# A layered transformer in one launch: expert row sends each followed by a copy, feed-forward weights quantised inside the expert stage, causal masks written by ScalarE

## What is computed

```
x = x + 0.5 * experts(ln(x))        # 8 routed experts, top 2 of them, and 2 shared; silu(x w1) * (x w3), then w2; hidden 256
x = x + attention0(ln(x))           # 16 heads of 8, 4 sequences of 1024, causal mask
x = x + 0.5 * experts(ln(x))        # the same weights
x = x + 0.5 * fp4_ffn(ln(x))        # gate, up, down with inner 352
x = x + attention1(ln(x))           # 16 heads of 64
x = x + 0.5 * fp4_ffn(ln(x))

def fp4_quant_dequant(x):           # blocks of 16 along the last dim; used on activations and on weights
    scale = max(max(|block|) / 6, 1e-12)
    return nearest_grid(|block| / scale) * sign(block) * scale   # grid 0 0.5 1 1.5 2 3 4 6
```

## Time and profile before

| what | us |
|---|---|
| median of three runs | 2107.71 |
| the profiled execution's own time | 2103.85 |
| its span in the profile | 2102.1 |
| of it: experts m1 (11.4 to 340) | 328.6 |
| attention0 (340 to 1016) | 676.0 |
| experts m2 (1016 to 1354.6) | 338.6 |
| feed-forward weights (1354.6 to 1373.5) | 18.9 |
| feed-forward f1 and the next norm (1373.5 to 1630) | 256.5 |
| attention1 (1630 to 1948) | 318.0 |
| feed-forward f2 and the end | 154 |

### The profile page before, as it was taken

How to read it: one execution, slowest core, us unless ns; L and a number is a source line. 1 busy time by engine, 2 the same in 40 slices (tenths; PEclk the granted TensorE clock), 3 DMA queues, 4 the chain that set the end, 5 groups by cost and what they waited for, 6 DMA issues and landing times. The chain is left out here.

```text
span 2102.1 us, 31391 instructions
## 1 busy us (share of the span) xinstructions
PE 1707.6 (81%) x10505; PEld 1173.3 (56%) x10505; DVE 1345.0 (64%) x2565; ACT 876.7 (42%) x1530; POOL 620.4 (30%) x669
## 2 busy tenths in 40 slices
PE   3987783999999999999399788257579999999475
PEld 2656661544544444443276676135347888888254
DVE  5534356877777777774463344579887666663796
ACT  2323331466666666667132333123224444444232
POOL 2355453211111011111226654213213333334132
PEclk9989996999999999999679898679879999999798
DMA  6022321111011111110402132100100000000000
GB/s 221 26 61 62 107 61 59 28 35 27 21 36 26 31 26 26 33 29 12 179 13 65 58 88 82 66 0 0 42 1 1 1 0 0 0 0 1 0 0 41
DMA packets 47705, 82.35 MB, mean 39 GB/s; under 512 B 10948, under 2 KB 32900, under 8 KB 46532
## 3 DMA queue, kind: packets, MB, share of 16 engines
q1 hardware_dynamic: 38500, 62.09, 10.3%
q0 software_dynamic: 9088, 18.76, 2.7%
HBM read 43.19 MB, written 31.22 MB: 35 GB/s over the span
## 5 line engine op out<-in xcount | busy, mean ns | idle before, releaser
L1824 DVE TENSOR_REDUCE z_parts<-z_pM 128x4 f32<-128x512 f32 x576 | 380.3, 687 | 144.6 <-PE z_pM L1576 78.3
L1745 ACT ACTIVATE z_Pr<-z_pE 128x512 f32<-128x512 f32 x576 | 326.4, 599 | 198.6 <-PE z_pE L1600 190.1
L1600 PE MATMUL z_pE<-z_QM,z_QK 128*128 128x512 f32 x576 | 265.1, 465 | 0.9 <-ACT z_Pr L1745 0.9
L1576 PE MATMUL z_pM<-z_KM,z_Q 128*128 128x512 f32 x576 | 247.7, 432 | 14.1 <-DVE z_parts L1824 7.6
L1928 POOL TENSOR_SCALAR_AFFINE_SELECT z_Pr<-z_Pr 128x512 f32<-128x512 f32 x128 | 81.5, 637 | 541.2 <-ACT z_Pr L1745 540.3
L1389 POOL TENSOR_TENSOR a_pm<-a_Pn,k_mask 128x512 f32<-128x512 f32 x128 | 132.4, 1059 | 271.4 <-PE a_pT L1227 153.4
L456 POOL DMA_INDIRECT slot_results<-m_yq,m_xq x156 | 150.8, 967 | 129.1 <-ACT m_yq L639 97.8
L1600 PEld LDWEIGHTS z_pE<-z_QM,z_QK 128*128 128x128 f32 x576 | 108.8, 190 | 134.3 <-ACT z_Pr L1745 103.0
L421 POOL DMA_INDIRECT slot_rows<-m_XN,m_dest x128 | 124.2, 970 | 162.7 <-issue 64.7
L1613 PE MATMUL z_pO<-z_Pr,z_V 128*9 128x512 f32 (+3 forms) x1536 | 159.7, 488 | 0.4 <-POOL z_Pr L1928 0.3
L1576 PEld LDWEIGHTS z_pM<-z_KM,z_Q 128*128 128x128 f32 x576 | 108.3, 188 | 80.5 <-DVE z_parts L1824 71.6
(11 more groups left out here) (286 smaller groups left out, 3769.5 us busy)
## 6 DMA issues: line engine op xcount, KB each, us to landing
slot_rows<-in_c_pad SPq DMA_DIRECT2D x2, 5070.0 KB, 23.8
m_xq<-slot_rows SPq DMA_DIRECT2D x38, 260.0 KB
z_QM<-z_Q SPq DMA_DIRECT2D x128, 64.0 KB, 2.0
z_KM<-z_QK SPq DMA_DIRECT2D x60, 128.0 KB, 2.4
m_raw<-in_gu SPq DMA_DIRECT2D x2, 2048.0 KB, 8.9
m_XN<-slot_results SPq DMA_DIRECT2D x8, 512.0 KB, 7.0
m_raw<-slot_results SPq DMA_DIRECT2D x8, 512.0 KB, 5.4
slot_results<-m_yq,m_xq POOLq DMA_INDIRECT x156
```

The costliest lines, as they stand in the source:

```text
L1576: last = mm(pM[n % 2][:, :].rearrange("p (h k) -> p h k", h=4), Q[G % 2][:, qt * P:(qt + 1) * P], KM[G % 2][:, :, kb * P:(kb + 1) * P], st ...
L1600: mm(pE[e % 3][:, :].rearrange("p (h c) -> p h c", h=4), QK[G % RING][:, kt * P:(kt + 1) * P], QM[half][:, :, q * P:(q + 1) * P], start=Tr ...
L1745: a.activation(Pr[j % 4][:, :, q * P:(q + 1) * P], pE[e % 3][:, :].rearrange("p (h c) -> p h c", h=4), ACT.Exp, scale=DH0 ** -0.5).then_in ...
L1824: v.tensor_reduce(parts[:, qt, kb, :], pM[n % 2][:, :].rearrange("p (h k) -> p h k", h=4), AX.X, ALU.max).then_inc(maxed, 1)
```

## The change

Four things change.

- **Sends.** Each of the 64 sends is followed by a small GpSimd copy (128x32, into `rest`), and GpSimd waits for it before the next send. The pace by `h_ready`, the six marks and the nine sends between the result sends are gone: all 32 sends of the first list, then all 32 of the second, then the result loop.
- **Rows between both lists' tags.** XN gets two more columns: id and gate of the second list ahead of the 128 numbers, those of the first behind. The second list's sends no longer wait until the first list's have landed. A send's size is the same.
- **Feed-forward weights inside m2.** SyncE loads them early in m2, VectorE does one of the eight quantising steps in each of the rounds r = 10 to 17 of the routed part, TensorE transposes behind its last pair, VectorE copies out ahead of the last adding back. The stage of their own is gone.
- **Masks by ScalarE.** From round G = 1 on, ScalarE copies `after_query` into the bank of a diagonal block (`fill_mask`) after exponential e = n - 2 (for n = 0 after e = 34 of the round before), once the block two earlier in that bank is reduced; the scores' matmul then accumulates onto it and the mask matmul is dropped (120 of 128).

```diff
-    PACE, FROM = (3, 5), 4
-    paced_by = lambda i: FROM + i * PACE[0] // PACE[1]
-    HEAD = 6
-        XN = s.sb("XN", [P, NT, ROW])
+        XN = s.sb("XN", [P, NT, ROW + 2])
+        XO, TAG = (0, 2), (D, 0)
+        rest, rested = s.sb("rest", [P, NT]), s.sem("rested")
+            F_FIRST, F_STEPS = 10, 8
...
+                if fp4:
+                    sp.wait_ge(w_low, 2)
+                    sp.wait_ge(f_step, 1)
...
+                    sp.dma_start(fw[:, 6 * P:], d["w_down"]).then_inc(f_loaded, 16)
...
+                if fp4:
+                    sp.wait_ge(f_step, 1 + F_STEPS)
                 load_back(1)
...
+                def send(k, sent):
+                    for t in range(NT):
+                        g_.indirect_dma_start(xs_dram, bass.IndirectOffsetOnAxis(dest[:, k, t:t + 1], 0), XN[:, t, 2 - XO[k]:2 - XO[k] + ROW], None).then_inc(sent, 16)
+
+                        g_.tensor_copy(rest[:, :], ids[:, 0, :]).then_inc(rested, 1)
+                        pool.wait_ge(rested, k * NT + t + 1)
...
-                for i in range(NT):
-                    pool.wait_ge(h_ready, paced_by(i))
-                    send(i)
-                pool.wait_ge(sent1, SENT)
-                g_.tensor_copy(XN[:, :, D:D + 1].bitcast(I32), ids[:, 1, :].unsqueeze(2)).then_inc(tagged, 1)
+                send(0, sent1)
                 pool.wait_ge(gates_ready, 2)
-                g_.tensor_copy(XN[:, :, D + 1:D + 2], g2[:, :].unsqueeze(2)).then_inc(tagged, 1)
+                g_.tensor_copy(XN[:, :, 1:2], g2[:, :].unsqueeze(2)).then_inc(tagged, 1)
                 pool.wait_ge(tagged, 4)
                 pool.wait_ge(dest_ready, 2)
-                for i in range(NT, IN_TIME):
-                    pool.wait_ge(h_ready, paced_by(i))
-                    send(i)
-                for i in range(IN_TIME, IN_TIME + HEAD):
-                    pool.wait_ge(*((q_turned, 1), (q_low, 1), (q_low, 2), (gu_ready, 1), (gu_ready, 2), (q_h, 1))[i - IN_TIME])
-                    send(i)
+                send(1, sent2)
                 for j in range(SLOT_TILES):
...
-                    if j % 2 == 0 and IN_TIME + HEAD + j // 2 < 2 * NT:
-                        send(IN_TIME + HEAD + j // 2)
...
+                if fp4:
+                    pe.wait_ge(f_step, 1 + F_STEPS)
...
+                    last.then_inc(f_turned, 1)
...
+                def quantise_weights(n):
+                    dve.wait_ge(f_step, 1 + n)
...
+                    if fp4 and F_FIRST <= r < F_FIRST + F_STEPS:
+                        quantise_weights(r - F_FIRST)
...
+                if fp4:
+                    dve.wait_ge(f_turned, 1)
+                    v.tensor_copy(fp4.wgT[:, :], tp[0][:, 0:INNER])
+                    v.tensor_copy(fp4.wuT[:, :], pm[:, 0:INNER])
+                    v.tensor_copy(fp4.wdT[:, :], gu[0][:, 0, 0:3 * D]).then_inc(f_step, 1)
...
-def load_fp4_weights(nc, C, s):
...
+                    if G and kb == qt:
+                        pe.wait_ge(filled, len(DIAG) * (G - 1) + DIAG.index(n) + 1)
                     last = mm(pM[n % 2][:, :].rearrange("p (h k) -> p h k", h=4), Q[G % 2][:, qt * P:(qt + 1) * P],
-                              KM[G % 2][:, :, kb * P:(kb + 1) * P], start=True, stop=(kb < qt), skip_group_check=True)
-                    if kb == qt:
+                              KM[G % 2][:, :, kb * P:(kb + 1) * P], start=(G == 0 or kb < qt), stop=(G > 0 or kb < qt), skip_group_check=True)
+                    if G == 0 and kb == qt:
                         last = mm(pM[n % 2][:, :], identb[:, :], after_query[:, :], start=False, stop=True, skip_group_check=True)
...
+                def fill_mask(G, n):
+                    act.wait_ge(maxed, NM * G + n - 1)
+                    a.activation(pM[n % 2][:, :], after_query[:, :], ACT.Copy).then_inc(filled, 1)
...
+                        if more and e + 2 in DIAG:
+                            fill_mask(G + 1, e + 2)
+                        if further and e + 2 == NM:
+                            fill_mask(G + 2, 0)
```

More of the change, by code:

```diff
@@ L293, in keep_busy, with moe_stage @@
         nc.tensor.matmul(bank, C["identb"][:, :], C["after_query"][:, :], start=True, stop=True, skip_group_check=True)
-def moe_stage(nc, C, name, Wt, turn):
+def moe_stage(nc, C, name, Wt, turn, fp4=None):
     X, ident, xh, xl, rank = C["X"], C["ident"], C["xh"], C["xl"], C["rank"]
@@ L318, in moe_stage @@
     COUNT2, GATES_AT = 6, 6
-    PACE, FROM = (3, 5), 4
-    paced_by = lambda i: FROM + i * PACE[0] // PACE[1]
-    IN_TIME = len([i for i in range(2 * NT) if paced_by(i) <= ND])
-    HEAD = 6
     with Scope(nc, name) as s:
-        XN = s.sb("XN", [P, NT, ROW])
+        XN = s.sb("XN", [P, NT, ROW + 2])
+        XO, TAG = (0, 2), (D, 0)
+        list_of = lambda j: j // LIST_TILES
+        rest, rested = s.sb("rest", [P, NT]), s.sem("rested")
         before, slot_ids = s.sb("before", [P, P]), s.sb("slot_ids", [1, LIST_TILES])
@@ L374, in moe_stage @@
         results = [po, tp[1]]
+        if fp4:
+            NB = (2 * 3 * P + INNER) // BLK
+            fw = s.sb("fw", [P, NB * BLK])
+            fwb = fw[:, :].rearrange("p (n b) -> p n b", b=BLK)
+            fy, fm = (raw[:, u * NB * BLK:(u + 1) * NB * BLK].rearrange("p (n b) -> p n b", b=BLK) for u in range(2))
+            fam, fsc, frs = s.sb("fam", [P, NB]), s.sb("fsc", [P, NB]), s.sb("frs", [P, NB])
+            f_loaded, f_step, f_turned = s.sem("f_loaded"), s.sem("f_step"), s.sem("f_turned")
+            F_FIRST, F_STEPS = 10, 8
         g_of, up_of = (lambda i: gu[0][:, i, :]), (lambda i: gu[1][:, i, :])
@@ L535, in turn_rows @@
                     for j in range(tiles_of(q)):
-                        last = nc.tensor.transpose(tp[0][:, j * P:(j + 1) * P], xq[q % RING][:, j, 0:D], ident[:, :])
+                        o = XO[list_of(q * QT + j)]
+                        last = nc.tensor.transpose(tp[0][:, j * P:(j + 1) * P], xq[q % RING][:, j, o:o + D], ident[:, :])
                     last.then_inc(q_turned, 1)
@@ L589, in _ @@
                     down(r, es.pop(r))
+                if fp4:
+                    pe.wait_ge(f_step, 1 + F_STEPS)
+                    pe.wait_ge(hT_kept, PAIRS)
+                    pe.wait_ge(q_low, QUADS)
+                    pe.wait_ge(q_h, PAIRS)
+                    for bank, i in ((tp[0], 0), (pm, 1)):
+                        for c, (a, k) in enumerate(IC):
+                            o = (3 * i + c) * P
+                            nc.tensor.transpose(bank[:, a:a + k], fw[0:k, o:o + P], ident[0:k, 0:k])
+                    for c, (a, k) in enumerate(IC):
+                        a = min(a, INNER - P)
+                        last = nc.tensor.transpose(gu[0][:, 0, c * D:(c + 1) * D], fw[:, 6 * P + a:6 * P + a + P], ident[:, :])
+                    last.then_inc(f_turned, 1)
             @block.scalar
@@ L854, in fp4_quantize @@
     s.st.count(v.scalar_tensor_tensor(s.y, s.m, MAGIC, s.y, ALU.max, ALU.subtract))
-def load_fp4_weights(nc, C, s):
[L859 to L886, removed]
-                nc.vector.tensor_copy(wgT[:, :], tp[0][:, 0:INNER])
-                nc.vector.tensor_copy(wuT[:, :], tp[1][:, 0:INNER])
-                st.done(nc.vector.tensor_copy(wdT[:, :], tp[2][:, 0:3 * D]))
-                nc.vector.memset(wdT[0:P - IC[2][1], 2 * D:3 * D], 0.0)
-            @block.tensor
-            def _(pe):
-                pe.wait_ge(quantised, 1)
-                for i in range(2):
-                    for c, (a, k) in enumerate(IC):
-                        o = (3 * i + c) * P
-                        nc.tensor.transpose(tp[i][:, a:a + k], raw[0:k, o:o + P], ident[0:k, 0:k])
-                for c, (a, k) in enumerate(IC):
-                    if k < P:
-                        a = INNER - P
-                    last = nc.tensor.transpose(tp[2][:, c * D:(c + 1) * D], raw[:, 6 * P + a:6 * P + a + P], ident[:, :])
-                last.then_inc(turned, 1)
-    return dict(wgT=wgT, wuT=wuT, wdT=wdT)
@@ L909, with __init__, ready @@
+class Fp4Weights:
+    def __init__(self, nc, C, s):
+        self.wgT, self.wuT, self.wdT = s.sb("wgT", [P, INNER]), s.sb("wuT", [P, INNER]), s.sb("wdT", [P, 3 * D])
+    def ready(self):
+        return dict(wgT=self.wgT, wuT=self.wuT, wdT=self.wdT)
 TP2 = 2
@@ L1474, in attention0_stage @@
         NM, NM0 = len(MU), 10
+        DIAG = [n for n in range(NM) if MU[n][0] == MU[n][1]]
         NJ, EU = 12, []
```

60 lines of the change are left out of this document (44 added, 16 removed).

## The result

The changed kernel took 2072.45 us (median of 4 runs, 2071.02 to 2079.82) beside 2107.44 for the kernel before (4 runs): a ratio of 0.984, 95% interval 0.982 to 0.987, so -35 us, where -27.9 had been forecast. The profiled execution took 2071.58 us against 2103.85: -32.3.

The account below looks back on a forecast made before the run. TensorE was taken to bound attention0 (643 of 676 us busy), the weights stage nobody. Weights -18.8, steps +3, sends -4.1 and masks -8 sum to -27.9: 2107.71 to 2079.8, so 2080 us, range 2070 to 2090, 8 in 10 within 2057 to 2108.

Parts of the forecast that it names:

- the likeliest case: Whole kernel: the forecast itself, 2080 us with its own range 2070 to 2090, chance 0.43.
- Weights, -18.8: Between m2 and f1: the weights stage goes, so the next stage's work moves up; -18.8 us.
- Steps, +3: m2's routed part: eight quantising steps on VectorE delay TensorE, four on the tight parity; +3 us, between 0 and 8.
- Masks, -8: attention0: dropped mask matmuls win 0.5 us a round at blocks 9, 14 and 27, over 15 rounds -8; bounds -28, +7.
- The case in which all slots are won: First rival, attention0: TensorE wins every mask slot, -28 for -8, giving 2060 us; chance 0.16.
- Sends, the cycle: GpSimd in m1 and m2: one send with its copy takes 1.54 us, bounds 1.44 to 1.84.
- second rival: GpSimd's sends in m1 and m2: cycle of 1.84 us makes TensorE wait for quad 4; +38.4, 2118 us; chance 0.15.
- The sum: Whole kernel: -18.8 + 3 - 4.1 - 8 = -27.9 us; 2076.0 profiled, 2079.8 as the median.
- Sends, against what: Routed experts: quad 8 at 209.4 against 211.69 in m1, -2.3 us; 1221.6 against 1223.41 in m2, -1.8.
- The even pace: Experts' shared part: whatever a more even pace wins is not cashed; TensorE only waits longer for quad 4.
- fourth rival: Experts: unseen releasers' waits go with the bursts, cycle 1.44, steady quads a little faster; -13 more, 2067 us; chance 0.08.
- Waits on unseen releasers gone during the sends: Sign for the sends step in the experts: waits whose releaser the profile doesn't show vanish while sends run.

Follow-up runs that it names:

- E1: The kernel before with the weights part of the change alone: ratio 0.9927 to the kernel before, -15.3 us.
- E11: E8 with a copy also behind each result send of quads 0 to 5: ratio 0.9791 to the kernel before, 2053.2 us.
- E4: Changed kernel with the first list's four result parts loaded back one behind each row load of quads 13 to 16: 0.9817 to the kernel before, 2054.3 us.
- E8: Changed kernel with E4's edit and the second list's last 5 row sends held back behind results of quads 0 to 4: 0.9719 to the kernel before, 2049.4 us.
- E7: Changed kernel with two copies in a row behind each send, each waited for: ratio 0.9997 to the kernel before, 2110.9 us.
- E6: Changed kernel without the copy behind each send: ratio 1.0325 to the kernel before, 2178.7 us.
- E2: The kernel before with the sends part alone (row layout, pace, copy behind each send): ratio 1.0023 to the kernel before, slower by 5.0 us.
- E9: The sends part alone on the kernel before, run once more on another chip: ratio 1.0026 to the kernel before.
- E5: The changed kernel run again, unaltered, on chip C: ratio 0.9828 to the kernel before, 2073.4 us.
- E10: The kernel before, pacing and layout kept, with only a waited-for copy behind each row send: ratio 1.0031 to the kernel before, slower by 6 us.

## Why the prediction was right, and where it was not

The time was forecast at 2080 and came out at 2072; the range of 2070 to 2090 held it, near its lower end, and the likeliest case is the one that came. Its terms:

- **Weights, -18.8:** m2's end to f1's is 18.3 us shorter, and E1 alone gives -15.3 for the term with the steps. The transposes and copies lie in VectorE's wait for the loaded results, as named (5.28 of 9.88 us are left).
- **Steps, +3:** from quad 8 to m2's end nothing was lost (126.9 us, 127.3 before), and E1 shows +1.8, within a spread of traces about as large. What the forecast missed was written in the earlier trace rows, for m1: a wait of 7 us for quad 13, which in m2 stands right behind the steps, and a delay in front of a wait for a transfer is mostly taken back there. With that wait removed, quads 8 to 13 of m2 took 5.1 us more than those of m1 in E11, 3.7 in E4 and 1.3 in E8.
- **Masks, -8:** -6.9 in the trace from first to last exponential, -5.8 over the stage, -10.0 alone with -6.5 to -13.8 around it. Blocks 0 and 2 cost what they win, as worked out. The case in which all slots are won is ruled out.
- **Sends, the cycle:** 1.54 taken, 1.48 measured. The term that was off is the start of a send behind the copy (0.34 for 0.28), with the copy 0.02 shorter. From the first send to the first result send 99.2 us were forecast; m2 took 95.6, 3.5 less, m1 96.4, 2.8 less, since three of its sends were longer. In m2 it shows, with a first send 1.3 us earlier from the stage's start; in m1 the first send came 0.9 later and the stretch behind quad 8 took 1.5 more than before, so that little is left. E7 confirms the price of a longer cycle: the second rival's mechanism is real, and only its size (1.84) didn't come. A shorter cycle is not worth the same: the prediction has its sum fall by 12.8 us for each 0.1, and E6 at 1.26 lost 105.
- **The sum:** -32.3 in the profiled execution against -27.9: m2 7.6 better (cycle 3.5, first send 1.3, steps 3.4, less 0.6 in between), m1 0.5 better, masks 2.2 worse, weights 0.5 and the rest 1.0 worse.
- **Sends, against what:** this step failed as a statement on the kernel. The gain was taken against quad 8 at 211.69, a mark that holds some 7 us of unseen waits. I named them and took them for part of the kernel. On chips B and E the same sends have none and quad 8 comes at 204.0 to 206.5; on B and D, where the kernel before runs at 2093 to 2094, the part alone costs 0.2 to 0.3% (E2, E9). That the part wins on the first chip is read from the two traces there; it was not run alone on such a chip. Here luck helped the forecast: the trace that it was summed against and the first result both have these waits in the kernel before. Without them the change is worth -20 to -25 us by the parts and by E4.
- **The even pace:** the fourth rival's reason (waits going with the bursts) fits the first chip's traces, though its time of 2067 needed more. "Waits on unseen releasers gone during the sends" held there but for 1.8 us, and not in E5. The shared part was done 5 us sooner and, as forecast, TensorE waited that much longer for quad 4.

**Copies beside VectorE's steps.** Of 128 copies two took 0.40 and 0.44 us and the others about 0.22, though two-input steps of VectorE run beside the first list's sends: copies hardly queued. Three sends of m1 grew, to 1.14 to 1.35 us, beside those steps, and none of m2: some 0.8 us in all, 1.2 with the two copies. The Trainium skill's "SBUF — State Buffer", section "Who interferes with whom", says that a DMA which seems held by a VectorE instruction is one whose descriptors GpSimd was kept from making. The three sends of m1 would fit that, but the sends of m2 kept their 0.98 us beside the same steps, so the trace doesn't show it; in size it didn't matter.

Still open: what the unseen waits are. They fall on VectorE and ScalarE while GpSimd's indirect sends follow each other, at 1.26 us apart and, on the first chip and on C, also at 1.48. They differ between chips: with the old sends the first chip's trace has them and those of B and E have none; with the new sends C's has 22 us in m1, the first chip's 1.8, those of B and D none. E6 and E7 were run on one chip only.

## What to carry to other kernels

Before a gain is counted against a mark in a trace, ask what in that mark is the kernel's and what comes and goes between chips: a wait on a releaser that the profile doesn't show is worth a second chip. Many indirect sends back to back can be paid for by the other engines (105 us in E6), and a copy of 0.22 us behind each can be the cheaper choice. Where such waits are absent, a later end of the sends is all that it brings (E2, E9, E10). Extra work belongs in front of a wait for a transfer that is late anyway, and the best edit found here was to remove such a wait: a load that nobody needs yet, moved behind the one that TensorE stands for.

## What was not expected of the hardware

- The same kernel before took 2093, 2094 and 2097 us on three chips, 2111 on a fourth and 2107 with the first result.
- While 64 indirect sends ran at 1.26 us apart (E6), unseen waits of ScalarE lasted up to 29.6 us and VectorE's up to 21.8. On the same chip at 1.48 with a copy between (E5) they lasted up to 3.7 us, at 1.75 with two copies (E7) there were none.
- A copy of 128x32 behind a send took 0.22 us and shortened the start of the next send to 0.28, for 0.30 behind another send; the second copy started 0.06 behind the first (E7).
